# The two-layer language tower with a pipeline of 64-position slots: everything but the top-k moves 16 positions towards it

## What is computed

```python
h = tok(x)                                          # 4 x 1024 tokens, 64 wide
h = h + toeplitz_attention(layernorm(h))            # three early stages, not touched
# product-key memory: 8 heads, 64 keys a side, 4096 entries a head
scores, idx = top_k(sim(q), 16)                     # of 64, on both sides
final_scores, pk = top_k(scores0 + scores1, 16)     # of the 16 x 16 sums
p = softmax(final_scores)
k = sum(p * keys_table[ind]); v = sum(p * values_table[ind])
h = h + causal_attention(q2, k, v) @ Wo             # 8 heads, 1024 x 1024
h = h + attention(layernorm(h), Wq, Wk)             # layer 1, one head
h = h + experts(layernorm(h), router, w1, w2)       # 8 experts, 2 chosen
```

## Time and profile before

| | |
|---|---|
| median of 3 runs | 3369.53 us (3368.63 to 3374.06) |
| the profiled execution | 3375.85 us, span 3374.0 us |
| PE, DVE busy | 2861.0 us (85%), 2759.2 us (82%) |
| ACT, POOL busy | 2057.2 us (61%), 2020.7 us (60%) |
| mean granted TensorE clock | 0.918 |

### The profile page before, as it was taken

One profiled execution on the slowest core, in us unless ns is written; L12 is line 12 of the kernel. 1 busy time (PEld: TensorE's weight loads), 2 busy tenths in 40 slices (PEclk: granted clock), 3 DMA queues, 4 the chain that ended last, 5 costly groups with the idle time before them and its releaser, 6 DMA issues. The chain is left out here.

```text
span 3374.0 us, 39544 instructions
## 1 busy us (share of the span) xinstructions
PE 2861.0 (85%) x9750; PEld 1346.6 (40%) x9750; DVE 2759.2 (82%) x10042; ACT 2057.2 (61%) x4514; POOL 2020.7 (60%) x2084
## 2 busy tenths in 40 slices
PE   5874466888989898989897979899988889899998
PEld 2442122343444343444353434344444344444434
DVE  7776987989898989897989998987979999966423
ACT  3222455676767676667677767676686767676322
POOL 3000477777777777776666777776757777767000
PEclk9986688899999989999898989999989999999978
DMA  1001122222222222222121212121212222221000
GB/s 41 26 10 46 28 59 69 58 71 63 66 64 64 64 64 65 61 65 61 49 65 43 78 52 76 49 76 43 68 45 63 66 71 55 64 61 52 7 0 3
DMA packets 85377, 179.61 MB, mean 53 GB/s; under 512 B 39991, under 2 KB 40922, under 8 KB 85150
## 3 DMA queue, kind: packets, MB, share of 16 engines
q0 software_dynamic: 66560, 135.40, 15.3%
q1 hardware_dynamic: 18590, 41.71, 3.9%
HBM read 175.92 MB, written 1.05 MB: 52 GB/s over the span
## 5 line engine op out<-in xcount | busy, mean ns | idle before, releaser
L1186 POOL DMA_INDIRECT mx_G<-in_kv_table,mx_slot_i x2048 | 1988.4, 971 | 1091.8 <-issue 602.7
L1214 PE MATMUL mx_acc<-mx_W,mx_table 128*128 128x512 f32 x2048 | 1109.5, 624 | 0.5 <-ACT mx_kvT L1415 0.4
L1571 DVE SCALAR_TENSOR_TENSOR mx_W<-mx_D,mx_W 128x512 f32<-128x512 f32 x1024 | 697.0, 681 | 261.8 <-ACT mx_W L1408 259.9
L1476 ACT ACTIVATE mx_GT<-mx_G,mx_slot_w 128x128 f32<-128x128 f32 x2048 | 759.2, 494 | 184.0 <-DMA mx_G<-in_kv_table,mx_slot_i 183.1
L1408 ACT ACTIVATE mx_W<-mx_D 128x512 f32<-128x512 f32 x1024 | 606.8, 593 | 183.2 <-PE mx_D L1204 178.8
L1214 PEld LDWEIGHTS mx_acc<-mx_W,mx_table 128*128 128x128 f32 x2048 | 411.7, 202 | 188.1 <-issue 113.9
L1204 PE MATMUL mx_D<-mx_U,mx_pick_b 96*128 96x512 bf16 x1024 | 411.5, 402 | 62.4 <-DVE mx_W L1571 61.0
L1432 ACT ACTIVATE mx_PT<-mx_area 128x512 f32<-128x512 f32 x480 | 246.5, 514 | 295.4 <-PE mx_area L1264 150.1
L1226 PE MATMUL mx_O<-mx_PT,mx_KVs 128*65 128x512 f32 (+3 forms) x768 | 312.6, 489 | 12.5 <-ACT mx_OT L1424 7.3
L1240 PE MATMUL mx_area<-mx_KTa,mx_QTa 64*128 64x512 f32 (+3 forms) x384 | 186.2, 567 | 151.1 <-DVE mx_mx_part L1806 123.6
L1788 DVE TENSOR_REDUCE mx_KVs<-mx_GT 128x128 f32<-128x2048 f32 x128 | 291.8, 2279 | 6.9 <-ACT mx_GT L1476 6.7
(11 more groups left out here) (376 smaller groups left out, 4363.6 us busy)
## 6 DMA issues: line engine op xcount, KB each, us to landing
mx_table<-in_kv_dense SPq DMA_DIRECT2D x64, 512.0 KB, 3.7
mx_G<-in_kv_table,mx_slot_i POOLq DMA_INDIRECT x2048
tz_table<-in_c_dft SPq DMA_DIRECT2D x1, 2048.0 KB, 8.9
tz_table<-in_c_idft SPq DMA_DIRECT2D x8, 256.0 KB, 2.6
out_h<-mx_xc SPq DMA_DIRECT2D x4, 256.0 KB, 3.7
mx_G<-in_c_pick SPq DMA_DIRECT2D x1, 528.0 KB
st_h<-in_tok_W,em_ids POOLq DMA_INDIRECT x32, 2.5
st_keys<-in_pk_keys SPq DMA_DIRECT2D x1, 512.0 KB, 4.0
```

The costliest lines, as they stand in the source:

```text
L1186: pool.indirect_dma_start(G[g % RING][:, r, :], None, a["kv_table"], bass.IndirectOffsetOnAxis(slot_i[n % 2][:, k, r:r + 1], 0))\
L1214: pe.matmul(acc[:, :], table[:, tile, :], W[c % TILE_RING][:, :], start=(tile == 0), stop=(tile == TILES - 1)).then_inc(applied, 1)
L1476: last = act.activation(GT[:, :, i], G[g % RING][:, i, :], ACT.Copy, scale=slot_w[n % 2][:, k, i:i + 1])
L1571: dve.scalar_tensor_tensor(W[c % TILE_RING][:, :], D_ps[c % 3][:, :], 0.0, W[c % TILE_RING][:, :], ALU.is_ge, ALU.mult).then_inc(w_done, 1)
```

## The change

Two kinds of uses are split: those of the top-k keep their positions, all others move 16 positions (`LEAD`) forward. In each engine's loop, v = q + 16 takes the place of q in everything but the top-k: dense tiles, weighted rows, attention, layer 1, experts. The loops end 16 positions earlier. In the small products' order one use of layer 1 (`l1y`, second half) goes from 19 to 20, since 19 - 16 = 3 belongs to a `sim`. POOL's and SP's programs are as they were; what they wait for moves.

```diff
-LAST = 17 * 64
+LEAD = 16
+LAST = 17 * 64 - LEAD
...
-def extra_uses(t):
+def topk_uses(t):
...
-        uses += [(5, ("U", t - 1, 2)), (6, ("U", t - 1, 3)), (40, ("post", t - 1, 0))]
+        uses += [(5, ("U", t - 1, 2)), (6, ("U", t - 1, 3))]
+    return uses
+
+def extra_uses(t):
+    uses = []
+    if 0 <= t - 1 < PAIRS:
+        uses += [(40, ("post", t - 1, 0))]
...
-            uses += [(10, ("l1y", b, 0)), (19, ("l1y", b, 1)), ...
+            uses += [(10, ("l1y", b, 0)), (20, ("l1y", b, 1)), ...
...
         for t in range(SLOTS):
-            for p, key in extra_uses(t):
-                self.x[key] = len(self.x)
-                self.x_at[(t, p)] = key
+            for shift, uses in ((0, topk_uses(t)), (LEAD, extra_uses(t))):
+                for p, key in uses:
+                    assert SLOT * t + p - shift not in self.x_at
+                    self.x_at[SLOT * t + p - shift] = key
+        for q in sorted(self.x_at):
+            self.x[self.x_at[q]] = len(self.x)
...
# PE, and the same in ACT's and DVE's loops
-            for q in range(SLOTS * SLOT):
-                c = q - SLOT
+            for q in range(SLOTS * SLOT - LEAD):
+                v = q + LEAD
+                c = v - SLOT
...
-                for use in area_uses(q - 2):
+                for use in area_uses(v - 2):
...
-                uses = area_uses(q)
+                uses = area_uses(v)
...
# DVE: top-k steps still go by q
-                t, p = divmod(q, SLOT)
+                t, p = divmod(v, SLOT)
...
                 n, r = divmod(q - 3, SLOT)
                 if 0 <= n < PAIRS:
                     for k in steps_at(r):
                         T(n, r // 32, k, mask_of_position)
...
-                n, r = divmod(q - 8 - SLOT, SLOT)
+                n, r = divmod(v - 8 - SLOT, SLOT)
```

More of the change, by code:

```diff
@@ L906, in extra_uses @@
         if s == 2:
-            uses += [(10, ("l1y", b, 0)), (19, ("l1y", b, 1)), (28, ("l2x", b, 0)), (29, ("l2x", b, 1)), (32, ("l2r", b))]
-    return sorted(uses)
+            uses += [(10, ("l1y", b, 0)), (20, ("l1y", b, 1)), (28, ("l2x", b, 0)), (29, ("l2x", b, 1)), (32, ("l2r", b))]
+    return uses
 class Counts:
@@ L1395, in _ @@
                     fill_area(uses[0])
-                if divmod(q, SLOT) in cnt.x_at:
-                    fill_extra(cnt.x_at[divmod(q, SLOT)])
+                if q in cnt.x_at:
+                    fill_extra(cnt.x_at[q])
                 if 0 <= c < PAIRS * SLOT and late:
@@ L1524, in _ @@
                     weigh_rows(t - 1, p // 8, p % 8)
-                for use in area_uses(q - 2):
+                for use in area_uses(v - 2):
                     if use in cnt.weigh and piece(use)[3]:
                         take_o(use)
-                for use in area_uses(q):
+                for use in area_uses(v):
                     if use in cnt.prob:
                         take_area(use)
-                key = cnt.x_at.get((t, p))
+                key = cnt.x_at.get(q)
                 if key is not None and key[0] not in ("post", "Y", "l1y", "l2r"):
@@ L1898, in experts @@
                 chain.link(dve.tensor_reduce(sq[:, t, :], yw[:, :, :].rearrange("p e d -> p d e"), AX, ALU.add))
-            for q in range(SLOTS * SLOT):
-                t, p = divmod(q, SLOT)
+            for q in range(SLOTS * SLOT - LEAD):
+                v = q + LEAD
+                t, p = divmod(v, SLOT)
                 if q == CONSTS:
                     constants()
-                uses = area_uses(q - 1)
+                uses = area_uses(v - 1)
                 if len(uses) == 2:
@@ L1908, in _ @@
                     experts(uses[0]) if uses[0][0] == "MY" else maxima(uses[0])
-                key = cnt.x_at.get(divmod(q - 1, SLOT))
+                key = cnt.x_at.get(q - 1)
                 if key is not None:
```

## The result

The changed kernel takes 3436.05 us (median of 4 runs, 3431.66 to 3436.99), the kernel before 3371.31 us beside it. The ratio is 1.0189, 95% interval 1.0172 to 1.0207: 64 us slower, where 19 were forecast and the range ended at 3413.

A forecast was written before the change was run, and what follows sets the result against it. The prediction took gathers, DVE and PE to bound successive stages of a slot; start -14.3, slots 2 to 5 +8.6 and slots 6 to 15 +25.1 gave +19.4 us on 3369.5, 3389 us, range 3349 to 3413.

The forecast's parts named there:

- Start, -14.3: Before slot 1: masks start about 21 us earlier, GpSimd's 14.3 us wait goes, the other 7.4 us are lost behind gathers.
- Phase, stage by stage: Top-k steps meet other work of each slot: +8.6 us over slots 2 to 5, +25.1 over slots 6 to 15.
- second stage: Positions v 16 to 39, both heads' scores: DVE's load falls by 5.7 us a slot, and the gathers take over as bound.
- gather pace: GpSimd's busy and issue time for gathers, 165.0 us a slot or 2.58 a position, taken as each stage's floor.
- third stage: Positions v 40 to 63, transposed scores and weighing: already full on PE, it gets 4.5 us more of top-k's products.
- the prediction's own sign: Slots 2 to 5 seen by their gathers keep 165 us; growth to 169 with GpSimd waiting would mean no lead.
- The X bank: PSUM bank shared by top-k and attention: Y now right ahead of sim in slots 2 to 15; counted 0, bounds 0 to 36.
- rival 3: The X bank stall shows each time, in slots 2 to 15: +19 + 36 = +55 us, 3425; chance 0.10.
- Rival 1, the gathers cover the phase: GpSimd's lead takes up PE's 4.5 us a slot: -27 us, 3342, or 3349 with half of slots 8 and 12; chance 0.20.
- Rival 4, the clock: PE, less busy in the first stage, runs at half clock there: +25 us more, 3414; chance 0.05.
- first stage: Positions v 0 to 15, no scores: DVE gets 5.5 us more a slot, PE loses 4.5; slot 3 stays at 41.2.

The follow-up runs named there:

- e1: The changed kernel with DVE's addition of heads moved ahead of the position's top-k steps, for every Y and l1y: 3389.71 us, ratio 1.0051.
- e6: The kernel before, with the gathers of the first two blocks not waiting for a dense mask: 3365.87 us, ratio 0.9984.
- e3: The kernel before, with 11 score products a slot (v 48 to 58) done twice, 8.2 us more PE work: 3488.26 us, ratio 1.0347.
- e16: The changed kernel as it is, run on a chip where the kernel before takes 3.94 to 3.97 ms: ratio 1.0030 to the kernel before there.

## Why the prediction was wrong

*The direction and its two causes were right.* Top-k's PE products came into the stage that PE fills, and more was lost there than the start brings. e1 is the kernel that my sum described, since I counted the shared bank at nothing: forecast +19.4 us, measured +16 to 18.

*Start, -14.3: right.* The first mask came at 371.8 us, as forecast. GpSimd's wait of 14.3 us is gone, and the 129th gather starts 13.5 us earlier (12.6 in e1). The two first masks are 20.7 us apart, and the first of slot 2 16.0 us (538.8 against 554.8; 14.8 in e1): the 5 us between are lost behind the gathers in slot 1, as the prediction had it. e6 confirms the rule by its own number.

*Phase, stage by stage: the loads were right, the floor was not.* DVE's second stage was to go from 61.8 to 56.1 us busy in slot 7, and is 56.5; its first was to be bound by DVE at 47.5, and takes 48.5 in e1; the third was to be PE's with 65.5, and takes 66.2. But I did not let the second stage fall under the gather pace (61.9), and it takes 56.6: the gathers bind a slot, not a stage. On the other side, the third stage of slot 8 takes 69.5 in e1 and not 65.5, so slot 8 gained 2 us and not 6.6. The errors cancel: slots 6 to 15 cost 22 us in e1, for 25.1 forecast. Slots 2 to 5 cost 7 (8.6 forecast), but not as the sum had it, with half of 4.3 in each. By the masks slot 2 costs 6.2, and slots 3, 4 and 5 cost 0.4, 0.3 and 0.3. By the gathers slots 1 to 5 of e1 keep 164.7 to 165.5 us, the prediction's own sign that the lead is there. It took up PE's 4.5 us whole in slots 3 to 5 (of e3's 8.2 it took half), and that the total is near 8.6 is luck.

*The X bank: this step failed.* The sum counted it at 0 us, and it cost 46. The prediction saw the place, the order of the products, what DVE does in between, and the 14 slots. It then took 0 of the 0 to 36 us, by the argument that PE waited 6 times in 16 before. That row is of a stage in which PE had slack, where it says nothing of a stage in which PE has none; the row that bears on it, PE 61.83 us busy of 62.0 in the third stage, stood in the earlier trace rows and spoke for the upper end. With 36 in its place the forecast would have been 3425. The text kept the 36 "for the range", and then the range ended at 3413, below rival 3's own 3425. And the upper end was itself too low: the wait is 33.1 us, about the 36, but it costs 46 us, for in eight of the 14 slots PE's clock is lower with it (0.95 against 1.00 in slot 7) and the same products take longer, 21 us in all there. That the wait comes near 36 is in part luck: 2.6 us was the mean of another place, and in the 14 slots it is 1.6 to 4.3.

*Rival 1, the gathers cover the phase:* true of slots 3 to 5 in e1, false of the rest, where slots 6 to 15 cost 22 us. *Rival 4, the clock:* it came, but not where I worked it out. The first stage of slot 3 has 0.84 before and after. It fell in the third stage, together with the waits, and in the first stages of slots 4 to 7, 10, 11, 14 and 15: slot 7's went from 1.00 to 0.87 (0.93 in e1), with PE 49.0 us busy where 44.8 less the 4.5 of top-k is 40.3. That is part of the 6.5 us by which that stage grew.

## What to carry to other kernels

Where a stage is full on one engine, price each new wait in it at its upper end, whatever the same wait cost elsewhere. When work is shifted against other work, list for each shared buffer who stands next in its order, and what the engine that frees it has to do first; freeing it ahead of that other work cost a few moved lines here and gave 46 us. That takes off the steps in between, and not the work that already stands ahead of the freeing engine. Read an engine that issues DMAs by busy time and issue time together: GpSimd set the pace of slot 3 before the change at 75% busy.

## What was not expected of the hardware

An fp32 product shows as two records; at 512 columns it takes 0.86 us and not the 0.43 us between records. In a stage full of products a pause that was 2.5 us longer came with 5.4 us more of time in slot 7, where the granted clock of the stage was 0.95 for 1.00; in slot 3, with the clock at 0.98 in both, a pause of 1.6 us cost 1.9.

Two chips took 3.94 to 3.97 ms for the kernel that takes 3.37 ms on the others. The page of e16, the changed kernel on one of them:

```profile
span 3951.9 us, 39542 instructions
PE 3049.0 (77%) x9750; PEld 1391.9 (35%) x9750; DVE 2799.0 (71%) x10042; ACT 2068.1 (52%) x4514; POOL 2023.5 (51%) x2084
```

Busy times of DVE, ACT and POOL are within 1.5% of those above; for them the difference is idle time. PE is 157 us longer busy, with a mean granted clock of 0.862 for 0.912. Among e16's waits are some that the profile lays to a remote event, a kind that no kernel shows on the other chips:

```profile
ACT mx_W L1421 <- remote: 179.3, 72, 7.9
PEld mx_D L1216 <- remote: 142.7, 34, 10.4
PE mx_D L1216 <- remote: 112.2, 31, 9.5
```

They come to 992 us over all engines. What these events are is open.
